# Third cross-attention on TensorE: keys and variance first, then weighing tiles and score tiles in turn

## The reference

```python
qx = ln(fp8_linear(x, wqx))            # 64 queries x 16 heads of 128, normed per head
kx, vx = split(ctx @ w_kv_x.T)          # 6272 keys x 8 groups of 128
kx = ln(kx)                             # per key and group: minus mean, over sqrt(variance)
p = softmax(qx @ kx.T / sqrt(128))      # per group: two heads x 64 queries = 128 columns
xout = p @ vx
```

## Time and profile before

| | |
|---|---|
| three runs, us | 1030.02, 1033.73, 1033.47 (median 1033.47) |
| profiled execution, span from first to last instruction | 1029.9 us |
| PE busy in the span | 981.5 us, 95% |
| DVE busy in the span | 715.1 us, 69% |
| granted TensorE clock, mean | 0.991 of full speed |
| stage 6, from its first weighing to its last | 475.0 to 904.2 us |

### The profile page before, as it was taken

The page is one execution under the profiler, slowest core; times in us unless marked ns, Lnnn a source line. Parts: engine busy times, 40 slices in busy tenths (PEclk is TensorE's granted clock), DMA queues, the critical chain, the costliest instruction groups (busy, mean ns, idle before and its releaser), DMA issues.

```text
span 1029.9 us, 20637 instructions
## 1 busy us (share of the span) xinstructions
PE 981.5 (95%) x7832; PEld 655.9 (64%) x7848; DVE 715.1 (69%) x1916; ACT 359.1 (35%) x629; POOL 162.3 (16%) x146
## 2 busy tenths in 40 slices
PE   9999999998799888999999999999999999898998
PEld 5676677675335444566777777777777777744555
DVE  5767767768799845886676867667676867843444
ACT  2333333334338832432333332433333332302211
POOL 0000000000210010342223223222332323000000
PEclk9999999999999999999999999999999999898999
DMA  8001001002239996940000000000000000232440
GB/s 311 25 22 42 21 20 38 23 5 84 73 115 195 190 337 250 338 170 1 1 1 1 1 0 0 0 0 0 0 0 0 0 1 2 82 144 82 159 192 4
DMA packets 66410, 75.41 MB, mean 73 GB/s; under 512 B 49329, under 2 KB 57265, under 8 KB 62513
## 3 DMA queue, kind: packets, MB, share of 16 engines
q1 hardware_dynamic: 66064, 74.57, 23.7%
q10 hardware_dynamic: 288, 0.07, 0.0%
HBM read 62.54 MB, written 0.07 MB: 61 GB/s over the span
## 4 chain that ended last, share of the span: by engine, by line
PE 77%; DVE 8%; issue 6%; DMA 3%; POOL 2%; ACT 2%; SPq 0%; POOLq 0%; DVEq 0%; PEld 0%; PEldq 0%
PE ps L2377 17%; PE ps L2271 15%; PE ps L2367 8%; PE ps L1570 8%; PE ps L1560 4%; PE ps L1581 4%; PE ps L1604 2%; PE ps L1616 2%; POOL x_sum L2902 1%; PE ps L515 1%; DVE vals L2097 1%; PE ps L2989 1%; PE ps L2294 1%; DMA wide<-vals 1%; PE ps L1590 1%
## 5 line engine op out<-in xcount | busy, mean ns | idle before, releaser
L2377 PE MATMUL ps<-vals,S 128*128 128x257 f32 x784 | 188.3, 384 | 0.7 <-ACT S L2834 0.7
L2271 PE MATMUL ps<-keysT,row_biases_sb 128*128 128x512 f32 (+1 forms) x416 | 185.4, 572 | 0.1
L2902 POOL TENSOR_TENSOR x_sum<-x_max,consts 128x4 f32<-128x4 f32 (+1 forms) x104 | 135.3, 1301 | 316.2 <-DVE x_max L2570 316.2
L2582 DVE SCALAR_TENSOR_TENSOR S<-ps,x_sum,keysT 128x128 f32<-128x128 f32 x392 | 110.9, 345 | 66.4 <-PE ps L2377 61.8
L2377 PEld LDWEIGHTS ps<-vals,S 128*128 128x128 f32 x784 | 143.1, 192 | 18.9 <-issue 1.0
L2834 ACT ACTIVATE S<-S 128x512 f32<-128x512 f32 (+1 forms) x104 | 62.6, 605 | 219.8 <-DVE S L2623 219.3
L2367 PE MATMUL ps<-x_q,x_keys 128*128 128x128 f32 x784 | 113.2, 286 | 0.0
L2271 PEld LDWEIGHTS ps<-keysT,row_biases_sb 128*128 128x128 f32 x416 | 75.9, 191 | 56.9 <-issue 51.0
L2367 PEld LDWEIGHTS ps<-x_q,x_keys 128*128 128x128 f32 x784 | 95.6, 191 | 0.1
L1570 PE MATMUL ps<-ring,S 128*128 128x512 f32 x196 | 92.3, 593 | 0.1
L2766 ACT COPY x_keys<-ps 128x512 f32<-128x512 f32 (+1 forms) x104 | 57.0, 548 | 65.4 <-PE ps L2367 32.8
(11 more groups left out here) (474 smaller groups left out, 1374.6 us busy)
## 6 DMA issues: line engine op xcount, KB each, us to landing
ring<-weights SPq DMA_DIRECT2D x24, 1024.0 KB, 7.0
keysT<-ctxT SPq DMA_DIRECT2D x2, 3136.0 KB, 14.9
vals<-ctxN SPq DMA_DIRECT2D x1, 6272.0 KB, 27.0
S<-ctxT SPq DMA_DIRECT2D x11, 512.0 KB, 4.0
ring<-weights SPq DMA_DIRECT2D x5, 768.0 KB, 5.9
keysT<-weights SPq DMA_DIRECT2D x1, 1792.0 KB, 8.9
keysT<-weights SPq DMA_DIRECT2D x1, 1536.0 KB, 12.1
row_biases_sb<-row_biases SPq DMA_DIRECT2D x1, 1416.0 KB, 9.4
```

The lines of the kernel that those rows point to most:

```text
L2271: ins = pe.matmul(ps[:, x2_key_bank(g, c), 0:width(c)], x2_wk[:, k, :], ctxT[:, k, span(c)], start=k == 0, stop=k == KT - 1)
L2377: ins = pe.matmul(bank(6, D + 1), S[:, a:a + TILE], ctx_and_ones[:, SUB * c + s, :], start=c == 0 and s == 0, stop=c == NC - 1 and s == su ...
L2582: ins = dve.scalar_tensor_tensor(S[:, a:a + TILE], ps[:, 3 + c % 2, 128 * s:128 * s + 128], x2_inv[:, c % 2, s:s + 1], x2_tile_const, ALU. ...
L2902: pool.tensor_tensor(x2_inv[:, c % 2, 0:n], x2_var[:, c % 2, 0:n], C("neg_half").broadcast_to([128, n]), ALU.pow)\
```

## The change

On PE alone. `scores` and `weigh` are cut into their waits and their tiles. In a step with both groups, for `c` from 0 to 11, the order becomes `keys(c + 3)`, `variance(c + 1)`, then the waits of `weigh(c)` and of `scores(c + 1)`, and then a tile of the weighing and a tile of the scores in turn. For `c` = 12 nothing changes. The other engines' lists, the semaphores and the buffers stay.

```diff
+            def weigh_and_score(weighed, scored, c):
+
+                weigh_wait(weighed, c)
+                scores_wait(scored, c + 1)
+                for s in range(subs(c)):
+                    weigh_tile(weighed, c, s)
+                    if s < subs(c + 1):
+                        score_tile(scored, c + 1, s)
...
             def step(scored, weighed, ahead, between={}):
 
                 for c in range(NC):
-                    if weighed is not None:
+                    both = weighed is not None and scored is not None and c + 1 < NC
+                    if weighed is not None and not both:
                         weigh(weighed, c)
                     if scored is not None:
                         if c + 3 < NC:
                             keys(scored, c + 3)
                         if c + 1 < NC:
                             variance(scored, c + 1)
-                            scores(scored, c + 1)
+                            if both:
+                                weigh_and_score(weighed, scored, c)
+                            else:
+                                scores(scored, c + 1)
```

More of the change, by code:

```diff
@@ L2352, in variance, with scores_wait @@
                 ins.then_inc(sem("x2_keys_var"), 1)
-            def scores(g, c):
+            def scores_wait(g, c):
                 pe.wait_ge(sem("x2_keys_ready"), g * NC + (c + 1))
@@ L2365, in scores, with score_tile, weigh_wait @@
                         pe.wait_ge(sem("x2_top"), g)
+            def score_tile(g, c, s):
+                ins = pe.matmul(ps[:, 3 + c % 2, 128 * s:128 * s + 128], x2_keys[:, c % 2, TILE * s:TILE * s + TILE], x2_q[:, :],
+                                start=True, stop=True)
+                if s == subs(c) - 1:
+                    ins.then_inc(sem("x2_scores_psum"), 1)
+            def scores(g, c):
+                scores_wait(g, c)
                 for s in range(subs(c)):
[L2367 to L2371, removed]
+                    score_tile(g, c, s)
+            def weigh_wait(g, c):
                 if c == 0 and not (isinstance(g, int) and g == 0):
@@ L2374, in weigh, with weigh_tile @@
                 pe.wait_ge(sem("x2_exp"), since("x2_exp", g * NC + (c + 1)))
-                for s in range(subs(c)):
[L2376 to L2379, removed]
+            def weigh_tile(g, c, s):
+                a = CHUNK * c + TILE * s
+                ins = pe.matmul(bank(6, D + 1), S[:, a:a + TILE], ctx_and_ones[:, SUB * c + s, :],
+                                start=c == 0 and s == 0, stop=c == NC - 1 and s == subs(c) - 1)
+                if s == subs(c) - 1:
+                    ins.then_inc(sem("x2_weighed"), 1)
+            def weigh(g, c):
+                weigh_wait(g, c)
+                for s in range(subs(c)):
+                    weigh_tile(g, c, s)
+            def weigh_and_score(weighed, scored, c):
[5 more added lines that the diff above has]
+                        score_tile(scored, c + 1, s)
             def turn_top(g):
```

## The result

The changed kernel takes 1203.44 us (median of four runs, 1201.43 to 1204.27), where the kernel before takes 1033.01: a ratio of 1.165, 95% interval 1.163 to 1.168. It is slower by 170 us. The forecast was 1176, from 1150 to 1210; the direction and the mechanism were right, the size was 27 us short.

The account below looks back on a forecast made before the run. PE was taken to bound the kernel before. 134 us for the ring and step edges plus 9 for the clock, on a span of 1029.9, gave 1173; the median's 3.6 above the span made 1176 us, range 1150 to 1210.

Parts of the forecast that it names:

- The ring: Steady chunks: weighing, `scale`, `low_half(c + 2)`, variance and next block wait in a circle, 6.10 us a period against 4.64.
- The sum per step: Step with both groups: chunk periods 17.36 us more, start 1.92 more, end 0.11 less; 19.2 a step, 134 over seven.
- The clock: Full in steady chunks, falling to 1.2 GHz at step ends: 1.26 us a step, 9 in all, at most 24.
- The evidence for a full clock in steady chunks: PE would be busy for 76% of steady chunks; stretches with 73% and 77% busy had kept the clock in full.
- the likeliest case's own range: 1158 to 1195 us: hidden loads and a mild fall below, the clock's 24 us and part of the switch bound above.
- the switch bound: Upper end for turns in a block: 0.12 us lost at each of seven switches, 72 us over 84 blocks.
- A switch between tiles: Turns between weighing and score tiles on PE: taken at nothing; hidden score loads could save 0.12 us a block.
- the border row: Profile row before the change, scores to weighing: the last score instruction takes 0.122 us like the seven before it.
- What costs nothing: Semaphores, DMA issues and the lists of SP, ACT and POOL: untouched; ACT or POOL join the ring only if needing over 4 us.
- Rival 1: The ring without a fall of the clock at step ends: 134 us more instead of 143, 1167 us; chance 0.22.
- Rival 2: The clock falls in steady chunks too, in every second of 63 periods: 53 us, 1229 us; chance 0.11.
- Rivals 3 and 4: 3: PE stays the bound, turns hide score loads, 1023 us, chance 0.04; 4: PE's order has no effect, 1033 us, 0.05.

Follow-up runs that it names:

- the pads: 63 matmuls without use a step, ahead of the variances of chunks 10, 11 and 12, added to the changed kernel: 1172.93 us, ratio 1.138.

## Why the prediction was right, and where it was short

- **The ring.** Right, link by link, and shown from both sides: taken apart on DVE's list, it goes (1059 and 1047 us); made 0.72 us longer, it adds 0.73 to 0.75 a chunk. Forecast 6.10 us, measured 6.12 in the step written out and 6.22 in the loop. The difference lies behind the variance: 0.36 us from the end of `low_half` to the first weighing tile where 0.28 was taken from a step that is written out and whose next tile is a score tile.
- **The sum per step.** 19.2 us were forecast without the clock; with the clock held up, the loop step is 78.5, 20.4 above 58.1. The 1.2 us between them are the nine steady periods, 56.1 us where 54.9 were forecast. The periods at their two edges came out 0.23 and 0.19 shorter (5.26 and 4.95) and the step's change 0.4 longer, which cancels. In all, 134 were forecast and 140 measured.
- **The clock.** That it holds in this kernel's steady chunks and falls at the steps' ends was right. Its price was the term that failed: 1.26 us a step, 9 in all, where the pads give back 30.5, more than the bound of 24. Two things in it were wrong. The count: one fall of 3.4 us a step was taken, 24 us at half speed in all; the step shown has three, 10.2 us together, the one after it has 13.7 us, and from the first `turn_top` to the last it is 78 us at half speed. The place: the price was read from the eight key matmuls behind a fall. In the step shown these lose nothing (717.42 to 720.85, 3.43 us, where 3.44 is the full-speed time); the falls come earlier, one in each of the last three blocks, and there the slow part lies in the ring: 4.33, 4.28 and (713.42 to 717.19) 3.77 us from block start to `scale`, where 2.70, 2.70 and about 2.2 were due, 4.8 us a step. PE's waits ahead of the three variances, 2.72, 2.97 and 2.22 us, stay about as long as they were; what a fall adds is the slower block.
- **The evidence for a full clock in steady chunks.** It was thinner than the prediction took it. The stretch with PE busy for 73%, 260 to 270 us, kept the clock in full in that trace, but the same untouched work shows 0.83 in the trace of the changed kernel, and 0.83 in five of the eight experiments, which leave it alone too. With the low half done twice, steady chunks at 70% busy saw it fall.
- **The range.** That 1203 lies in 1150 to 1210 is in part luck. It is above the likeliest case's own range, 1158 to 1195, and the room above 1195 was left for costly switches, which cost nothing. The terms named for the upper end (15 us more for the clock, 12 for a sixth of the switch bound) also add up to 1203 and not to 1195; without the switches they give 1191.
- **A switch between tiles.** Taken at nothing, and it is nothing: 2.72 us a block in the changed kernel, 1030.93 us with the turns alone. The pull-ahead of weight loads that the Trainium skill describes (TensorE: Matmul & The Clock Gate, "Part 2: What happens when you issue a matmul") gave none of the 0.12 us a block that it could have given. That agrees with the border row.
- **What costs nothing.** ACT, POOL and the DMAs stayed out of it, as the waits from 475 to 1080 us show: `scale` waits for the weighing alone, and `low_half` for ACT's squares 3 times, 1.2 us in all.
- **The rivals.** Rival 1 (no fall at the steps' ends, 1167) is what the kernel with pads runs like, 1173. Rival 2, at 1229 us, is as near to 1203 as the forecast is, so the time alone does not exclude it. The trace does: 650 to 690 us has PE busy for 80% and the clock in full, and no steady period in the stage is longer than 6.31 us. Rivals 3 and 4 are excluded by the 77 new waits.

No version of the study is faster than the kernel before: the turns in the old place equal it, and there PE has no idle time that an order could remove.

## What to carry to other kernels

Before moving work on the engine that is the bound, list for each waiting instruction what its releaser's engine has ahead of it in its own list; if one of those waits for what was moved, close the ring and add up its parts. Engines are free of each other only as long as that sum is under the period of the bound. A dose (an instruction done twice) shows cheaply which it is: nothing where there is slack, its whole length per period where there is a ring. And when a change leaves TensorE idle, count the falls over the whole idle stretch and not one for it, and price each on the block that it meets, as far as that block lies on the path.

## What was not expected of the hardware

The clock's fall cost a path on which TensorE was idle for a good part of the time. With PE busy for 60% of 690 to 700 us, the clock was at half for three stretches of 3.4 us in the next 17, each over a block that the ring waited for, and 63 matmuls without use a step made the kernel 30.5 us faster, 2.5% of it. With PE busy for 80% from 650 to 690 us it had stayed in full.
